# x's rows for the last sums: sixteen indexed transfers issued by GpSimd in place of four direct loads issued by SyncE

## The chip, the cores and the metric

One core of one Trainium2 chip runs the whole program. The metric is the device time of one execution in microseconds (us). A core has TensorE (PE, matmuls; PEld is its weight loads), VectorE (DVE), ScalarE (ACT), GpSimd (POOL) and SyncE (SP). SP here only issues transfers, and POOL issues some beside its arithmetic. All transfers run on 16 DMA engines that the core's queues share.

## The reference

A layer of graph attention over 2048 nodes of width 256, with 8 heads of width 32, in float32:

```
h   = relu(layernorm(x))                                   # source rows
hs, ht = masked layernorms of h and of h_target, with scale and bias
q, k, v = ht @ Wq + bq (divided by sqrt 32), hs @ Wk + bk, hs @ Wv + bv
p   = softmax over the sources of q.k where adj != 0
ht  = layernorm(ht + (p @ v) @ Wo + bo), masked
out = x + ht + gelu(ht @ W1) @ W2
```

What the change is about is the first term of the last line: the raw rows of x are wanted a second time, at the very end.

## The kernel before, in words

The 2048 targets are cut into 4 chunks of 512 columns (4 tiles of 128 rows, `TILES`). There are three stages.

**Projections.** x and h_target come in, are normalised and turned, and give keys, queries and values. The buffer of x is given to other tensors afterwards. The keys are split into a high and a low part for the matmuls, and copies of keys, values and queries are saved to memory for a rare general path that a flag chooses (the flag is 0 here).

**Attention.** For every chunk, group of 4 heads and tile of sources, PE makes scores, DVE masks them into a ring `probs` of 12 buffers, ACT takes the exponential, and PE multiplies by the values. POOL adds some of the exponentials up (`add_up`) and loads the mask's rows (`load_adj`). The sums of a chunk go to memory, come back packed, are inverted by DVE (`invert`), are stored again, and are then broadcast by SP over the partitions into `inverse` (`spread_inverse`, L394 to L403: 2 transfers of 256 KB, one per group of heads, in which each of 4 source rows is repeated for 32 partitions). For the last chunk DVE multiplies the context by it (`divide_last`, L1153), and PE's `attend(LAST)` (L1465) waits for that product.

**The last stage.** For each chunk c in turn PE runs `widen` (8 steps of 6 matmuls, W1), `turn_y` (transposes for the next chunk), `narrow` (8 steps of 6 matmuls, W2), and within `widen(c)`, at its third step, `turn_out(c - 1)` (L1577: 8 transposes of the finished chunk before). `attend(LAST)` stands between `narrow(0)` and `widen(1)`. ACT takes the two gelus of each step; DVE makes the low part of each (`split_gelu`, L1099), and between them the normalisation of later chunks (`y_stats`, `y_root`, `y_apply`), `join(c)` (L1104) for which `turn_out(c)` waits, and `finish(c)` (L1112), which adds x's rows from the buffer `xr` and writes `result`. Every engine runs its list in the order in which it is written, and the waits are on counted semaphores. `finish(0)` stands in DVE's list behind the second `split_gelu` of chunk 1. `narrow(1)` waits for `finish(0)`, as both use the accumulator `acc`.

`xr` holds one chunk's rows: 128 partitions by 4 tiles by 256 values, over the space of the keys, and so SP loads it first when the copies of the keys are saved (L467 to L469), then again behind the stores of each chunk (L480). At the end of POOL's list, behind the attention, stand two multiplications and additions over the last chunk of the residual (`make_residual(LAST, ...)`, L564), which wait for the low half of chunk 0's activations (`y_lo_out`), and then only the reading of the flag.

Of the kernel before, what the change touches and what calls it, by code (L numbers as in the profile page):

```python
# [5 lines left out]
F32 = mybir.dt.float32  # L6
F32R = mybir.dt.float32r
BF16 = mybir.dt.bfloat16
I32 = mybir.dt.int32
U16 = mybir.dt.uint16  # L10
ACT = mybir.ActivationFunctionType
ALU = mybir.AluOpType
AX_X = mybir.AxisListType.X

P = 128
# [8 lines left out]
TILES = CHUNK // P  # L24
# [8 lines left out]
def graph_attention(nc, x, adj, nodemask, h_target, ln1_scale, ln1_bias, Wq, bq, Wk, bk, Wv, bv, Wo, bo,  # L33
                    ln2_scale, ln2_bias, W1, W2, out):
    S, D = x.shape
    FF = W1.shape[1]
    NCH = S // CHUNK
    ST = S // P
# [6 lines left out]
    NT = NCH * GT  # L45
# [16 lines left out]
    x_rows = x.rearrange("(n p) d -> p n d", p=P)  # L62
# [13 lines left out]
    with ExitStack() as ctx:  # L76
        def sb(name, shape, dt, scope=ctx):
            return scope.enter_context(nc.sbuf_tensor(name, shape, dt))

        def sem(name):  # L80
            return ctx.enter_context(nc.semaphore(name))
# [30 lines left out]
        largest_all = sb("largest_all", [P, 1], F32)  # L112
        largest_one = sb("largest_one", [1, 1], F32)
        flag = sb("flag", [1, 1], I32)
        sums = sb("sums", [P, NCH, PACK], F32)
        inverses = sb("inverses", [P, NCH, PACK], F32)
        wo = sb("wo", [P, DC, D], F32)
# [11 lines left out]
        with ExitStack() as late:  # L129
            g_hi = sb("g_hi", [P, FC, CHUNK], F32R, late)  # L130
            g_lo = sb("g_lo", [P, FC, CHUNK], F32R, late)
            xr = sb("xr", [P, TILES, D], F32, late)
            out_T = sb("out_T", [P, DC, CHUNK], F32, late)
            g_full = sb("g_full", [P, 2, CHUNK], F32, late)
            result = sb("result", [P, TILES, D], F32, late)
# [43 lines left out]
        with ExitStack() as late:  # L179
            yT_hi = sb("yT_hi", [P, DC, CHUNK], F32R, late)  # L180
            yT_lo = sb("yT_lo", [P, DC, CHUNK], F32R, late)
            yT = [sb(f"yT{i}", [P, DC, CHUNK], F32, late) for i in range(2)]
        probs = sb("probs", [P, RING, 2, CHUNK], F32, att)
        added_up = sb("added_up", [P, PAIRS, 2, CHUNK], F32, att)
        sums_wide = sb("sums_wide", [P, CHUNK], F32, att)
# [19 lines left out]
        columns_made = sem("columns_made")  # L205
        node_row_in = sem("node_row_in")
        made = sem("made")
        beta_masked = sem("beta_masked")
        nodes_made = sem("nodes_made")
        row_tested = sem("row_tested")  # L210
# [25 lines left out]
        kept = sem("kept")  # L236
# [13 lines left out]
        used = sem("used")  # L250
# [32 lines left out]
        x_again = sem("x_again")  # L283
# [3 lines left out]
        summed = sem("summed")  # L287
# [31 lines left out]
        def rows_of(c):  # L319
            return slice(c * TILES, (c + 1) * TILES)  # L320
# [50 lines left out]
        def _(sp):  # L371
# [92 lines left out]
                    sp.dma_start(v_saved, V[:]).then_inc(kept, 16)  # L464
            store_sums(LAST, 1)
            pack_sums(LAST)
            sp.wait_ge(used, NT)  # L467
            sp.wait_ge(kept, 16 * 3)
            sp.dma_start(xr[:], x_rows[:, rows_of(0), :]).then_inc(x_again, 16)  # L469
            spread_inverse(LAST)  # L470
            def store_last(ts, ds, results):
                sp.wait_ge(summed, TILES * LAST + results)
# [2 lines left out]
            for c in range(LAST):  # L475
                for half in range(2):
                    ts = slice(half * TILES // 2, (half + 1) * TILES // 2)
                    sp.wait_ge(summed, TILES * c + (half + 1) * TILES // 2)
                    sp.dma_start(out_rows[:, rows_of(c), :][:, ts, :], result[:, ts, :]).then_inc(stored, 16)
                sp.dma_start(xr[:], x_rows[:, rows_of(c + 1), :]).then_inc(x_again, 16)  # L480
                if c == LAST - 1:
                    sp.wait_ge(ht_kept, 16)
                    sp.wait_ge(q_kept, 32 * NCH)
                    general = load_flag(sp, "sp")
# [33 lines left out]
        def _(pool):  # L518
            def load_adj(c, t):
                n = c * TILES + t  # L520
                if n >= 2:
# [8 lines left out]
            pool.dma_start(vec_rows[NV - ST:NV, :], nodemask.rearrange("(n p) -> n p", p=P)).then_inc(nodes_in, 16)  # L530
            pool.dma_start(node_row[:], nodemask.rearrange("(o s) -> o s", o=1).to_broadcast([P, S])
                           ).then_inc(node_row_in, 16)
            pool.wait_ge(x_in[2], 16)
            load_adj(0, 0)
            pool.wait_ge(x_in[3], 16)
# [28 lines left out]
            def make_residual(c, step):  # L564
                h = htn[:, rows_of(c), :]
                if step == 0:
                    if c == 0:
                        pool.wait_ge(rest_made, 2)
                        pool.wait_ge(ht_kept, 16)
                    nc.gpsimd.tensor_tensor(h, h, gamma1_row[:, None, :].to_broadcast(wide), ALU.mult  # L570
                                            ).then_inc(residual, 1)
                else:
                    pool.wait_ge(residual, 2 * c + 1)
                    nc.gpsimd.tensor_tensor(h, h, rest_row[:, None, :].to_broadcast(wide), ALU.add
                                            ).then_inc(residual, 1)
# [23 lines left out]
            pool.wait_ge(y_lo_out, DC)  # L599
            make_residual(LAST, 0)  # L600
            make_residual(LAST, 1)

            general = load_flag(pool, "pool")
            with pool.If(general):
# [257 lines left out]
        def _(dve):  # L862
# [247 lines left out]
                                            ).then_inc(joined, 1)  # L1110

            def finish(c):  # L1112
                dve.wait_ge(x_again, 16 * (c + 1))
                if c:
                    dve.wait_ge(stored, 32 * c)
                for t in range(TILES):
                    n = c * TILES + t
                    dve.wait_ge(out_turned, 2 * c + t // 2 + 1)
                    nc.vector.scalar_tensor_tensor(out=result[:, t, :], in0=acc4[:, t, :], scalar=nodes[:, n:n + 1],
                                                   in1=xr[:, t, :], op0=ALU.mult, op1=ALU.add).then_inc(summed, 1)  # L1120

            def finish_last():
                def join_part(d, at, width):
                    ts = slice(at, at + width)
                    nc.vector.tensor_tensor(out_T[:, d, ts], acc[:, d, ts], yT[LAST % 2][:, d, ts], ALU.add
                                            ).then_inc(joined, 1)

                def result_part(t, d):
                    n, ds = LAST * TILES + t, slice(d * P, (d + 1) * P)
                    nc.vector.scalar_tensor_tensor(out=result[:, t, ds], in0=slot4[0][:, t, ds], scalar=nodes[:, n:n + 1],  # L1130
                                                   in1=xr[:, t, ds], op0=ALU.mult, op1=ALU.add).then_inc(summed, 1)

                dve.wait_ge(out_turned, 2 * LAST)
                dve.wait_ge(narrowed, DC * LAST + 1)
                join_part(0, 0, CHUNK)
                dve.wait_ge(x_again, 16 * NCH)
                dve.wait_ge(stored, 32 * LAST)
                dve.wait_ge(out_turned, 2 * LAST + 1)
                for t in range(TILES):
                    result_part(t, 0)  # L1140
                dve.wait_ge(narrowed, DC * NCH)
                for half in range(2):
                    join_part(1, half * CHUNK // 2, CHUNK // 2)
                for half in range(2):
                    dve.wait_ge(out_turned, 2 * LAST + 2 + half)
                    for t in range(half * TILES // 2, (half + 1) * TILES // 2):
                        result_part(t, 1)
# [530 lines left out]
```

## Time and profile before

| | us |
|---|---|
| median of 3 runs | 491.21 (490.66 to 491.3) |
| span of the profiled execution | 488.1 |
| PE busy in the span | 472.1 (97%) |
| DVE busy | 418.4 (86%) |
| ACT busy | 376.5 (77%) |
| POOL busy | 305.6 (63%) |

The profile shows one execution, from its first to its last instruction: the span. What lies around it (start and end of the program) is in the median and not in the span, and no time of its own is given for the profiled execution beside its span, so the median less the span, 3.1 us, stands for that part. PE is busy nearly throughout; its granted clock is 0.998 over the span. A busy figure is an average over all stages. The change is in the last stage, which begins at about 376 us.

### The profile page before, as it was taken

The numbers are of one execution on the slowest core, as the hardware profiler recorded it, in microseconds if no ns is written. First come the engines' busy times: TensorE is split into PE (matmuls) and PEld (weight loads), VectorE is DVE, ScalarE is ACT, GpSimd is POOL, SyncE is SP. The second block draws the span as 40 slices with busy tenths as digits, with TensorE's granted clock in tenths as the row PEclk, the third lists the DMA queues.
The fourth block names the chain that finished last, engine by engine and source line by source line (L and its number), as shares of the span: only waits on it lengthen the run. The fifth ranks groups of instructions, "written<-read, shape, count | busy, mean of one in ns | idle before, by whom it ended". The sixth has DMA issues, their size and how long they took to land.

```text
span 488.1 us, 10628 instructions
## 1 busy us (share of the span) xinstructions
PE 472.1 (97%) x4366; PEld 243.2 (50%) x4366; DVE 418.4 (86%) x631; ACT 376.5 (77%) x462; POOL 305.6 (63%) x152
## 2 busy tenths in 40 slices
PE   3999989999999999999999999999999999999995
PEld 1557533343333333343333333343435888888884
DVE  6889499999999999999999999999997977566243
ACT  4887979998998998998998998999995571727150
POOL 1000019977998999999999998999998300000000
PEclk9999999999999999999999999999999999999999
DMA  8997879925432673232763400500000100202021
GB/s 231 243 217 133 157 216 385 346 47 109 172 69 47 76 173 58 44 52 50 77 177 57 77 2 3 186 35 1 2 2 1 46 33 13 87 1 86 1 87 45
DMA packets 53775, 46.93 MB, mean 96 GB/s; under 512 B 35486, under 2 KB 46652, under 8 KB 53212
## 3 DMA queue, kind: packets, MB, share of 16 engines
q1 hardware_dynamic: 51216, 37.30, 28.7%
q0 software_dynamic: 2480, 8.92, 10.4%
q8 instruction: 35, 0.57, 0.5%
q14 instruction: 16, 0.13, 0.1%
q10 hardware_dynamic: 28, 0.01, 0.0%
HBM read 31.93 MB, written 14.81 MB: 96 GB/s over the span
## 4 chain that ended last, share of the span: by engine, by line
PE 72%; DVE 11%; issue 9%; ACT 4%; POOL 3%; DMA 1%; DVEq 0%; POOLq 0%
PE acc L1434 18%; PE slot L1419 16%; PE acc L1452 8%; DVE probs L1044 8%; PE slot L1536 3%; PE slot L1534 3%; PE slot L1535 3%; PE slot L1322 3%; PE acc L1571 2%; PE acc L1573 2%; PE acc L1572 2%; PE slot L1485 2%; POOL added_up L554 2%; DVE stats L865 1%; PE slot L1342 1%
## 5 line engine op out<-in xcount | busy, mean ns | idle before, releaser
L1044 DVE SCALAR_TENSOR_TENSOR probs<-maskT,slot 128x1024 f32<-128x1024 uint16 x256 | 298.0, 1217 | 6.1 <-PE slot L1419 5.7
L759 ACT ACTIVATE probs<-probs 128x1024 f32<-128x1024 f32 x256 | 266.8, 1057 | 22.3 <-DVE probs L1044 4.8
L554 POOL TENSOR_TENSOR added_up<-added_up,probs 128x1024 f32<-128x1024 f32 x96 | 226.8, 2411 | 0.2
L1434 PE MATMUL acc<-probs,V 128*32 128x512 f32 x1024 | 136.3, 604 | 1.8 <-DVE q_lo_staged L970 1.8
L1452 PE MATMUL acc<-probs,ones 128*32 128x256 f32 x1024 | 77.0, 379 | 0.0
L1452 PEld LDWEIGHTS acc<-probs,ones 128*32 128x32 f32 x1024 | 33.3, 110 | 72.8 <-issue 71.2
L1419 PE MATMUL slot<-q_hi,k_hi 32*128 32x512 f32 x512 | 64.4, 493 | 0.9 <-DVE probs L1044 0.3
L823 ACT ACTIVATE g_full<-slot 128x512 f32<-128x512 f32 x32 | 19.3, 602 | 45.2 <-issue 30.0
L1419 PEld LDWEIGHTS slot<-q_hi,k_hi 32*128 32x128 f32 x512 | 24.5, 181 | 59.1 <-DVE probs L1044 54.4
L551 POOL TENSOR_TENSOR added_up<-probs 128x1024 f32<-128x1024 f32 x16 | 38.1, 2406 | 24.9 <-ACT probs L759 15.0
L1419 PE MATMUL slot<-q_lo,k_hi 32*128 32x512 f32 x512 | 51.8, 391 | 0.0
L1419 PE MATMUL slot<-q_hi,k_lo 32*128 32x512 f32 x512 | 51.3, 389 | 0.0
L1434 PEld LDWEIGHTS acc<-probs,V 128*32 128x32 f32 x1024 | 20.3, 108 | 48.7 <-issue 46.0
L523 POOL DMA_DIRECT2D adj_raw<-in_adj x16 | 8.9, 559 | 49.5 <-DMA maskT<-adj_raw 38.0
L1101 DVE TENSOR_TENSOR g_lo<-g_full,g_hi 128x512 fp32r<-128x512 f32 x32 | 23.0, 718 | 17.4 <-ACT g_hi L824 17.3
L1419 PEld LDWEIGHTS slot<-q_lo,k_hi 32*128 32x128 f32 x512 | 24.7, 183 | 4.7
L1534 PE MATMUL slot<-yT_hi,w_hi 128*128 128x512 f32 x64 | 25.6, 399 | 0.0
L1536 PE MATMUL slot<-yT_hi,w_lo 128*128 128x512 f32 x64 | 25.0, 390 | 0.0
L1535 PE MATMUL slot<-yT_lo,w_hi 128*128 128x512 f32 x64 | 24.9, 389 | 0.0
L1419 PEld LDWEIGHTS slot<-q_hi,k_lo 32*128 32x128 f32 x512 | 24.9, 184 | 0.0
L824 ACT ACTIVATE g_hi<-slot 128x512 fp32r<-128x512 f32 x32 | 19.1, 597 | 0.0
L1571 PE MATMUL acc<-g_hi,w_hi 128*128 128x512 f32 x48 | 18.9, 394 | 0.0
(144 smaller groups left out, 496.6 us busy)
## 6 DMA issues: line engine op xcount, KB each, us to landing
adj_raw<-in_adj POOLq DMA_DIRECT2D x16, 512.0 KB, 5.5
htn<-in_L_gnn_h_target SPq DMA_DIRECT2D x4, 512.0 KB, 7.4
ht_saved<-htn SPq DMA_DIRECT2D x1, 2048.0 KB, 8.1
k_hi_saved<-k_hi SPq DMA_DIRECT2D x1, 2048.0 KB, 10.2
k_lo_saved<-k_lo SPq DMA_DIRECT2D x1, 2048.0 KB, 14.5
v_saved<-V SPq DMA_DIRECT2D x1, 2048.0 KB, 8.9
inverse<-inverse_saved SPq DMA_DIRECT2D x8, 256.0 KB
maskT<-in_L_gnn_W SPq DMA_DIRECT2D x2, 1024.0 KB, 6.4
```

What stands on the lines that cost most here:

```text
L551: nc.gpsimd.tensor_tensor(added_up[:, pair], at(ADDED[0]), at(i), ALU.add).then_inc(added, 1)
L554: nc.gpsimd.tensor_tensor(added_up[:, pair], added_up[:, pair], at(i), ALU.add).then_inc(added, 1)
L759: nc.scalar.activation(p, p, ACT.Exp).then_inc(exped, 1)
L1044: nc.vector.scalar_tensor_tensor(out=probs[:, u % RING], in0=m, scalar=-HALF_EDGE, in1=slot[u % SLOTS][:], op0=ALU.add, op1=ALU.min).then_ ...
L1101: nc.vector.tensor_tensor(g_lo[:, f, :], g_full[:, f % 2, :], g_hi[:, f, :].bitcast(F32), ALU.subtract).then_inc(gelu_lo, 1)
L1419: mm = pe.matmul(slot[(PAIRS * k + j // 2) % SLOTS][:, j % 2, :], keys_part[head, g, i * P:(i + 1) * P], queries_part[head, g, :], start=( ...
L1434: mm = pe.matmul(acc[HD * j:HD * j + HD, 0, :], V[:, i, h * HD:(h + 1) * HD], probs[:, (PAIRS * k + j // 2) % RING, j % 2, :], start=(i == 0),
L1452: mm = pe.matmul(acc[HD * j:HD * j + HD, 1, ts], ones[:], probs[:, (PAIRS * k + j // 2) % RING, j % 2, ts], start=first and not half, stop ...
L1534: pe.matmul(dst, w1_hi[:, d, fs], yT_hi[:, d, :], start=(d == 0), stop=False)
L1535: pe.matmul(dst, w1_hi[:, d, fs], yT_lo[:, d, :], start=False, stop=False)
L1536: mm = pe.matmul(dst, w1_lo[:, d, fs], yT_hi[:, d, :], start=False, stop=(d == DC - 1))
L1571: pe.matmul(dst, w2_hi[:, f, ds], g_hi[:, f, :], start=(f == 0), stop=False)
```

## The change

`xr` becomes four times as large and holds all 16 tiles of x. It leaves the space of the keys for that of the `probs` ring. POOL makes a table of row numbers at the start (`iota`), and behind its two residual steps issues one indexed transfer for each tile of 128 rows, each with one row number per partition. SP's first load and its two waits, and its three loads behind the stores, are gone. `finish(0)` waits for all sixteen transfers; the later chunks and `finish_last` wait for no load.

```diff
+        row_index = sb("row_index", [P, ST], U32)
...
-            xr = sb("xr", [P, TILES, D], F32, late)
...
             yT = [sb(f"yT{i}", [P, DC, CHUNK], F32, late) for i in range(2)]
+            xr = sb("xr", [P, ST, D], F32, late)
...
             pack_sums(LAST)
-            sp.wait_ge(used, NT)
-            sp.wait_ge(kept, 16 * 3)
-            sp.dma_start(xr[:], x_rows[:, rows_of(0), :]).then_inc(x_again, 16)
             spread_inverse(LAST)
...
-                sp.dma_start(xr[:], x_rows[:, rows_of(c + 1), :]).then_inc(x_again, 16)
...
+            nc.gpsimd.iota(row_index[:], pattern=[[P, ST]], base=0, channel_multiplier=1).then_inc(index_made, 1)
             pool.wait_ge(x_in[2], 16)
             load_adj(0, 0)
...
             make_residual(LAST, 0)
             make_residual(LAST, 1)
+
+            pool.wait_ge(index_made, 1)
+            pool.wait_ge(used, NT)
+            pool.wait_ge(kept, 16 * 3)
+            for n in range(ST):
+                pool.indirect_dma_start(
+                    out=xr[:, n, :], out_offset=None, in_=x,
+                    in_offset=bass.IndirectOffsetOnAxis(ap=row_index[:, n:n + 1], axis=0)).then_inc(x_again, 16)
...
             def finish(c):
-                dve.wait_ge(x_again, 16 * (c + 1))
+                if c == 0:
+                    dve.wait_ge(x_again, 16 * ST)
...
-                                                   in1=xr[:, t, :], op0=ALU.mult, op1=ALU.add).then_inc(summed, 1)
+                                                   in1=xr[:, n, :], op0=ALU.mult, op1=ALU.add).then_inc(summed, 1)
...
             def finish_last():
...
-                                                   in1=xr[:, t, ds], op0=ALU.mult, op1=ALU.add).then_inc(summed, 1)
+                                                   in1=xr[:, n, ds], op0=ALU.mult, op1=ALU.add).then_inc(summed, 1)
...
-                dve.wait_ge(x_again, 16 * NCH)
```

## Rows read from the trace of the kernel before

**Rows 1.** The profile's first page, busy time of each engine
```profile
PE 472.1 (97%) x4366; PEld 243.2 (50%) x4366; DVE 418.4 (86%) x631; ACT 376.5 (77%) x462; POOL 305.6 (63%) x152
```
**Rows 2.** Busy time by stretch: PE, PEld, DVE, ACT, POOL, PE's clock, DMA share, GB/s
```profile
410.00:430.00 20.00, 20.00 (x99) 16.80 (x98) 14.18 (x31) 11.38 (x20) 0.00 (x0) 1.00 0.17 54
382.00:384.00 2.00, 2.00 (x11) 1.74 (x11) 2.00 (x3) 2.00 (x4) 0.00 (x0) 1.00 0.75 233
398.65:404.10 5.45, 5.45 (x26) 4.52 (x25) 2.55 (x4) 3.39 (x6) 0.00 (x0) 1.00 0.25 96
316.00:320.00 4.00, 4.00 (x52) 1.57 (x52) 4.00 (x5) 3.82 (x6) 4.00 (x2) 1.00 0.28 102
```
**Rows 3.** Waits from 395 to 488 us: engine, line <- releaser: total, times, longest
```profile
DVE g_lo L1101 <- ACT g_hi L824: 17.3, 25, 1.8
DVE context L1158 <- DMA inverse<-inverse_saved: 2.0, 1, 2.0
```
**Rows 4.** What touches the tile xr: durations in ns min/median/max, first and last start
```profile
L480 SPq DMA_DIRECT2D xr<-in_x x3: 500/503/505, 418.4 to 465.5; - x3
L469 SPq DMA_DIRECT2D xr<-in_x x1: 401/401/401, 380.8 to 380.8; - x1
...
DMA to landing us min/median/max: 3.9/3.9/4.2
```
**Rows 5.** POOL's instructions in order: start, duration, line, operation
```profile
2.58 0.56 POOL L531 DMA_DIRECT2D node_row<-in_nodemask  x1
12.90 0.53 POOL L523 DMA_DIRECT2D adj_raw<-in_adj  x1 [9.76 <-DMA xs<-in_x]
...
26.87 0.53 POOL L523 DMA_DIRECT2D adj_raw<-in_adj  x1 [11.18 <-DMA maskT<-adj_raw]
...
387.43 2.40 POOL L574 TENSOR_TENSOR htn<-htn,rest_row 128x1024 f32<-128x1024 f32 x1
```
**Rows 6.** The line of POOL's direct loads, durations in ns
```profile
L523 POOL DMA_DIRECT2D adj_raw<-in_adj x16: 530/570/593, 12.9 to 256.0; - x16
```
**Rows 7.** SP's queue in order of time
```profile
395.55 0.61 SPq L396 DMA_DIRECT2D inverse_saved<-inverses  x1
397.44 1.14 SPq L402 DMA_DIRECT2D inverse<-inverse_saved  x2
```
**Rows 8.** The page's list of transfers: size, median us to landing
```profile
out<-result SPq DMA_DIRECT2D x7, 256.0 KB, 2.2
```
**Rows 9.** DVE in order of time, 388 to 418 us
```profile
388.80 1.57 DVE L1101 TENSOR_TENSOR g_lo<-g_full,g_hi 128x512 fp32r<-128x512 f32 x1
...
392.66 0.69 DVE L1101 TENSOR_TENSOR g_lo<-g_full,g_hi 128x512 fp32r<-128x512 f32 x1
...
404.78 1.29 DVE L1158 TENSOR_TENSOR context<-context,inverse 128x512 f32<-128x512 f32 x2 [2.02 <-DMA inverse<-inverse_saved]
...
411.52 1.28 DVE L1109 TENSOR_TENSOR out_T<-acc,yT 128x512 f32<-128x512 f32 x2
...
416.28 1.65 DVE L1119 SCALAR_TENSOR_TENSOR result<-acc,nodes,xr 128x256 f32<-128x256 f32 x4
```
**Rows 10.** PE and ACT in order of time
```profile
393.94 0.59 ACT L824 ACTIVATE g_hi<-slot 128x512 fp32r<-128x512 f32 x1
...
395.03 0.39 PE L1534 MATMUL slot<-yT_hi,w_hi 128*128 128x512 f32 x1
...
408.16 3.61 PE L1485 MATMUL slot<-wo,context 128*128 128x256 f32 x16
...
414.36 1.04 PE L1581 MATMUL acc<-ident,out_T 128*128 128x128 f32 x8
...
424.21 0.48 PE L1571 MATMUL acc<-g_hi,w_hi 128*128 128x512 f32 x1
```
**Rows 11.** DVE beside POOL's load of 26.87 us
```profile
26.85 0.16 DVE L876 TENSOR_TENSOR newton<-rstd 128x4 f32<-128x4 f32 x1
27.05 0.16 DVE L878 SCALAR_TENSOR_TENSOR newton<-spread,newton 128x4 f32<-128x4 f32 x1
```

More of the change, by code:

```diff
@@ L9 @@
 I32 = mybir.dt.int32
+U32 = mybir.dt.uint32
 U16 = mybir.dt.uint16
@@ L207, in graph_attention @@
         made = sem("made")
+        index_made = sem("index_made")
         beta_masked = sem("beta_masked")
```

## The prediction, made before the changed kernel was run

> **What bounds the kernel now.** I looked first at the busy shares: PE is busy 472.1 of 488.1 us and no other engine comes near [rows 1]. Then at the stage that the change touches, by stretches: from 410 to 430 us PE is busy all 20.00 us at full clock, DVE 14.18, ACT 11.38, POOL 0.00, and the DMA engines 0.17 of the time [rows 2]. So PE sets the pace there, each instruction behind the last, and a change counts only if it makes PE wait or takes a wait from it. Then the waits of that stage: DVE waits for ACT in small pieces, 25 times, 17.3 us in all, and once 2.0 us for the broadcast of the inverse sums; nobody waits for `xr` [rows 3, 4]. What I need beyond that is how far each thing that PE waits for is ahead of PE, and for that I read single instructions in order of time.
>
> **What the change removes.** SP's four issues cost it 0.40 us once and 0.50 us three times, their data lands 3.9 us after the issue, and nothing waits for it [rows 4]. The first stands at 380.8, and SP's next work begins at 395.55, when the sums are inverted [rows 4, 7]; the three others stand behind stores and in front of an idle queue. The two waits taken from SP and the two kinds of wait taken from DVE were satisfied long before. So the removal gives 0.0 us on PE's path. What hides it is SP's idle time, and if that were gone it would be 0.5 us for each load at the most.
>
> **What it adds early.** One table-making instruction on POOL behind the issue of 2.58 us. POOL then idles 9.76 us before its load of 12.90 [rows 5]. The trace has no such instruction; it makes 16 values per partition, and the bounds are 0 and the 2.40 us of a POOL instruction over 1024 values [rows 5]. Either way it is hidden: 0.0 us. The new place of `xr` costs nothing that I can find, as the `probs` ring is dead when POOL reaches the transfers, and their waits (`used`, `kept`, the table) are met by then.
>
> **What it adds late.** POOL ends its residual step at 387.43 + 2.40 = 389.83 and now issues 16 transfers of 128 rows of 1 KB, 128 KB each. Only the reading of the flag is queued behind them, at the end of the program. The trace has no indexed transfer. Its nearest rows are POOL's direct loads over 128 partitions, 0.57 us each, one right behind the other where two are issued [rows 5, 6]; this is the lower end. The upper end is 2.40 us, POOL's instruction over a whole tile [rows 5]. An indexed transfer must fetch a number per row and make an address of it, which the direct one doesn't, and so I take twice the direct one, 1.1 us: nearer the row of its own kind. Then the last is issued at 389.83 + 16 x 1.1 = 407.4, and with some 2.5 us to land (2.2 for a store of 256 KB [rows 8]) all of x is there at 409.9. `finish(0)` starts at 416.28 [rows 9], so this adds no wait. It could even start later: PE needs its 1.65 us done only at 424.21, when `narrow(1)` starts [rows 9, 10], that is a start at 422.6. The wait begins to cost when POOL's pitch exceeds (422.6 - 2.5 - 389.83) / 16 = 1.89 us.
>
> **What these transfers collide with.** At 397.44 SP issues the broadcast of the inverse sums, 2 x 256 KB, and the wait for it ends at 404.78 [rows 7, 9]. Its data moves from about 398.65 to 404.1 at 96 GB/s with a DMA share of 0.25; the same broadcast one chunk earlier shows 102 GB/s and 0.28 over 4 us, while x's direct load of the same size shows 233 GB/s and 0.75 [rows 2]. A share that stays at a quarter, at a steady rate, in a transfer that nothing else disturbs, reads as 4 of 16 engines that are full, rather than 16 that idle three quarters of the time. The Trainium skill says how this comes: on the page "DMA: Bandwidth & Descriptors", section "Rules for kernel authors", a transfer whose outermost dimension has fewer than 16 entries is confined to at most that many engines, and here the outermost has 4 heads. The share of 0.25 agrees. If the rule did not hold here, x would run in the idle three quarters and the collision would cost nothing, which is the rival "hidden" below.
>
> With full engines x's packets delay it. Per busy engine the broadcast moves 96 / (16 x 0.25) = 24 KB per us, x's load 233 / (16 x 0.75) = 19.4. An indexed transfer puts 128 / 16 = 8 KB on each engine: 0.33 us at the first rate, 0.41 at the second. At one per 1.1 us this is 0.30 to 0.38 of each engine's time, all through the broadcast. Its 5.45 us become 5.45 / 0.70 = 7.8 to 5.45 / 0.62 = 8.8, which is 2.35 to 3.35 us more. Those four engines run at the higher rate, so I take 2.4, and 0.2 for the small store of 395.55 ahead of it, which now stands among x's packets (bounds 0 and 0.4, one transfer's share): the broadcast lands D = 2.6 us later.
>
> Who waits? DVE, which waits already, is late by all of D. Its list from 404.78 to 412.80 (`divide_last`, statistics, the root, `join(0)`) has no gap, so `join(0)` ends at 412.80 + D, and `turn_out(0)` on PE, at 414.36 now, has 1.56 us to spare [rows 9, 10]. `attend(LAST)`, at 408.16, with the product ready at 406.07, has 2.09 to spare: the earlier stall is 2.6 - 2.09 = 0.5 and is part of the later one. PE loses D - 1.56 = 1.0 us, and as PE runs without a gap from there to the end, the end moves by it. DVE's own lateness is then made good in its gaps [rows 3].
>
> **The sum.** 488.1 + 0.0 (removed) + 0.0 (table) + 0.0 (wait of `finish(0)`) + 1.0 (collision) = 489.1 of span, and with the 3.1 us around it 492.2; from the median, 491.21 + 1.0 = 492.2. For the collision's bounds: at the lower end of 0.57 us per transfer POOL is done at 399.0 and x is through at about 401, so the broadcast shares its engines for only 2.3 us at a share of 0.7: D = 1.7, cost 0.1. At 1.5 us the share is 0.22 to 0.27, D is 1.5 to 2.0, cost 0 to 0.5. At 1.1 us and the slower packets D is 3.4 to 3.8, cost 1.8 to 2.2. Less than nothing is not to be had, as nothing on PE's path goes.
>
> **The rivals.**
>
> Hidden: the collision costs less than the 1.56 us that PE has in hand, because a DMA engine fills the gaps of one queue with packets of the other, or because the pitch is near the direct one or near 1.5 us. For it: even the direct load of x shows engines busy only 0.75. Against it: the four engines of the broadcast show no gap. Time 491.2, not slower than before; it decides for D under 1.56 us. Chance 0.22.
>
> Late x: POOL needs more than 1.89 us for each transfer, and then `finish(0)` holds `narrow(1)`. At 2.1 us: 389.83 + 33.6 + 2.5 = 425.9, 3.3 us after 422.6, time 494.5. At the upper end of 2.40: 430.7, 8.1 us late, 499.3. For it: software makes these transfers and it must read an index for each row. Against: it would be over three times the direct load. The Trainium skill speaks for this rival too: "DMA: Bandwidth & Descriptors", "Anatomy of one DMA", gives a transfer from GpSimd a fixed 2.0 us beside its bytes; if the fixed part were paid one after the other, the sixteen would be an estimated 32 us by that page and land late. The direct issues here are over after 0.57 us each [rows 6], which speaks against its being paid so on POOL. Chance 0.12.
>
> Port: POOL and DVE keep each other from memory. The low part of a gelu takes 1.57 us at 388.80 beside POOL's residual step, against 0.69 at 392.66 [rows 9]. If sixteen indexed transfers do the same, DVE's chain from 390.37 to the split at 392.66 and the gelu that ends at 394.53 has only 0.5 us in hand before the matmul of 395.03 [rows 10]. One split that is 0.88 late costs 0.4 us, and if each of DVE's eight two-input instructions there is held so, 8 x 0.88 - 0.5 = 6.5 us. Against it: tiny instructions of DVE keep their 0.16 us and their pitch of 0.20 beside POOL's direct load at 26.87 [rows 5, 11]. Time 491.6 to 497.7. The Trainium skill has the rule on the page "SBUF — State Buffer", section "Who interferes with whom": a VectorE instruction with two inputs in SBUF contends with a GpSimd instruction that reads it. An indexed transfer reads its row numbers there, the direct one reads nothing. Chance 0.06.
>
> Gain: the freed queue and the loads that don't stand beside the last chunks' stores bring 0.6 us or more. I find no instruction that waits for either. Time 490.6. Chance 0.05.
>
> **How the numbers follow.** The forecast (a broadcast late, PE held at `turn_out(0)` for 1.0 us) has 0.55, with its own range of 491.4 to 493.4. Its time is 492.2. About 0.2%, 1.0 us, is what a measurement of this kernel can tell from no change, and the forecast lies on that line: I give 0.33 of its 0.55 to slower and 0.22 to the same. Hidden adds 0.21 to the same and 0.01 to faster, late x 0.11 to slower and 0.01 to the same, port 0.05 and 0.01, gain 0.05 to faster. Together: faster 0.06, same 0.45, slower 0.49. The range is 490.8 to 495.3: it holds the forecast, hidden, and the mild half of late x and port.
>
> **What would show it.** The wait of DVE's `divide_last` for the broadcast grows from 2.0 to some 4.6 us, and the DMA share between 398.6 and 406 rises from 0.25 to about 0.6. POOL shows 16 instructions of about 1.1 us from 389.8 to 407. PE shows a first gap of about 0.5 us before `attend(LAST)` and another before `turn_out(0)`, 1.0 us together, and none before `narrow(1)`. A pitch above 1.9 us and a gap in front of `narrow(1)` would prove late x; splits of more than 0.7 us between 390 and 407, port; a broadcast that lands at 404.8 to 406.3, hidden. I'm wrong outright if PE stalls in front of anything else, or the time falls below 490.8.

## The result, and the profile after

The changed kernel takes 492.68 us (median; 491.84 to 495.31), the kernel before in the same session 490.66 (490.11 to 493.08). The ratio is 1.0039, 95% interval [1.0022, 1.0056]: slower by 1.9 us. The forecast was 492.2 and 1.0 us, so the cost is 0.9 us above it.

The profile shows where it goes, if one thing is taken off first. In this execution everything was already 0.29 us late before POOL's first indexed transfer: the low part of a gelu that began at 388.80 [rows 9] begins at 389.09. That belongs to the attention, which the change doesn't touch, and is called the offset below. Every "later" is after it is taken off.

POOL in order of time, changed kernel (start, duration, instruction, idle time before it):
```profile
387.72 2.41 POOL L574 TENSOR_TENSOR htn<-htn,rest_row 128x1024 f32<-128x1024 f32 x1
390.28 1.29 POOL L607 DMA_INDIRECT xr<-in_x,row_index  x1 [0.16 <-issue]
...
394.79 1.59 POOL L607 DMA_INDIRECT xr<-in_x,row_index  x1 [0.30 <-issue]
...
400.83 0.95 POOL L607 DMA_INDIRECT xr<-in_x,row_index  x1 [0.30 <-issue]
402.08 0.96 POOL L607 DMA_INDIRECT xr<-in_x,row_index  x1 [0.30 <-issue]
...
411.14 0.95 POOL L607 DMA_INDIRECT xr<-in_x,row_index  x1 [0.30 <-issue]
```
Sixteen transfers in 20.86 us from the first start to the last, 1.39 from one to the next on the mean and 1.26 during the broadcast; a good fifth of it is a gap of 0.30 us behind each.

SP's queue, then two stretches: 410 to 430 as in [rows 2], and the eight microseconds of the broadcast:
```profile
395.85 0.61 SPq L399 DMA_DIRECT2D inverse_saved<-inverses  x1
398.35 1.14 SPq L405 DMA_DIRECT2D inverse<-inverse_saved  x2
```
```profile
410.00:430.00 20.00, 19.68 (x96) 16.35 (x95) 14.92 (x41) 11.37 (x20) 1.78 (x2) 1.00 0.15 48
399.30:407.30 8.00, 8.00 (x37) 6.63 (x36) 2.20 (x4) 3.03 (x5) 5.90 (x7) 1.00 0.48 157
```
The broadcast is issued 398.35 - 397.44 - 0.29 = 0.62 us later [rows 7], since it waits for the small store to land. From its issue to the start of `divide_last` it then takes 9.71 us where it took 7.34, 2.37 more, so its 5.45 us of data have become some 7.8, in a stretch whose DMA share is 0.48 and not 0.25 [rows 2].

DVE, then PE, in order of time:
```profile
389.09 1.58 DVE L1109 TENSOR_TENSOR g_lo<-g_full,g_hi 128x512 fp32r<-128x512 f32 x1
...
398.73 0.69 DVE L1109 TENSOR_TENSOR g_lo<-g_full,g_hi 128x512 fp32r<-128x512 f32 x1 [0.29 <-issue]
...
408.06 1.29 DVE L1166 TENSOR_TENSOR context<-context,inverse 128x512 f32<-128x512 f32 x2 [5.00 <-issue]
...
414.92 1.28 DVE L1117 TENSOR_TENSOR out_T<-acc,yT 128x512 f32<-128x512 f32 x2
...
418.45 1.65 DVE L1128 SCALAR_TENSOR_TENSOR result<-acc,nodes,xr 128x256 f32<-128x256 f32 x4
```
```profile
409.50 3.69 PE L1493 MATMUL slot<-wo,context 128*128 128x256 f32 x16 [0.83 <-DVE context L1166]
...
416.26 1.09 PE L1589 MATMUL acc<-ident,out_T 128*128 128x128 f32 x8 [0.33 <-DVE out_T L1117]
...
426.17 0.48 PE L1579 MATMUL acc<-g_hi,w_hi 128*128 128x512 f32 x1
```
`divide_last` begins D = 408.06 - 404.78 - 0.29 = 2.99 us later. PE gets two gaps, 0.83 before `attend(LAST)` and 0.33 before `turn_out(0)`. (They make up less than PE's lateness, because a matmul otherwise begins before the modelled end of the one before it: `attend(LAST)` begins 409.50 - 408.16 - 0.29 = 1.05 us later and `turn_out(0)` 1.61.) It reaches `narrow(1)` 426.17 - 424.21 - 0.29 = 1.67 us later, which is inside the interval of the ratio (1.1 to 2.7 us). `finish(0)` waits for nothing, and no gap stands in front of `narrow(1)`.

### The profile page after: what moved, and what is told of

It reads as the page before. It is cut to its first block, busy times and chain, and to the rows that moved or that the text cites. A ratio compares the mean times of both kernels' runs of the same rounds, so it can differ in the third digit from the quotient of the medians.

```text
span 490.3 us, 10641 instructions
## 1 busy us (share of the span) xinstructions
PE 473.4 (97%) x4366; PEld 243.4 (50%) x4366; DVE 418.5 (85%) x631; ACT 376.5 (77%) x462; POOL 323.1 (66%) x169
## 4 chain that ended last, share of the span: by engine, by line
PE 66%; DVE 15%; issue 10%; ACT 4%; POOL 3%; DMA 2%; DVEq 0%; SPq 0%; POOLq 0%
PE acc L1442 18%; PE slot L1427 16%; PE acc L1460 8%; DVE probs L1052 8%; PE slot L1330 3%; POOL added_up L554 2%; PE slot L1544 2%; PE slot L1542 2%; PE slot L1543 2%; DVE stats L873 2%; PE slot L1493 1%; PE acc L1580 1%; PE acc L1581 1%; PE acc L1579 1%; PE slot L1350 1%
## 5 line engine op out<-in xcount | busy, mean ns | idle before, releaser
L607 POOL DMA_INDIRECT xr<-in_x,row_index x16 | 17.2, 1077 | 4.7 <-issue 4.7
```

## The experiments

All ran timed against the kernel before. D is the lateness of `divide_last` and "PE's loss" that of `narrow(1)`, both with that run's own offset taken off (read at the gelu of 388.80 [rows 9], in experiment 2 at that of 392.66; at that of 388.80 both of its figures would be 0.07 us more). In the texts on record, where letters stand, A is the collision of x's packets with the broadcast, and C a second mechanism that the traces brought up: late updates of TensorE's counters.

**1. The changed kernel again.** No edit.

> The changed kernel again, as the measure for its neighbours. Theory A (the indexed transfers share the four engines of the inverse broadcast; DVE's divide_last, join(0) and then PE are late): ratio to before 1.004 (1.003 to 1.005), divide_last starts about 408.0 against 404.8, x lands before finish(0) wants it. Rival B (POOL's sixteen instructions themselves disturb DVE or the program as a whole, wherever they stand): the same time, so it isn't told apart here.

Measured: 492.51 against 491.16, ratio 1.0037 [1.0020, 1.0053]. D is 3.23, PE's loss 1.87. The effect repeats.

**2. Direct transfers in the place of the indexed ones.**
```diff
-                pool.indirect_dma_start(out=xr[:, n, :], ..., in_offset=...)
+                pool.dma_start(xr[:, n, :], x_rows[:, n, :]).then_inc(x_again, 16)
```


> In place of the sixteen indexed transfers POOL issues sixteen direct ones of the same rows, at the same place. Theory A: only the traffic matters. POOL is done in 16 x 0.57 = 9.1 us, at 399.5, and 2 MB are through by about 401, so the broadcast (data from about 399) shares its engines for 2 us at a share near 0.7: it lands 1.4 us later for that and the small store 0.6 us later, D = 2.0, PE loses 0.4: ratio 1.001 (1.000 to 1.002). Theory that it is the indexing that costs (reading row numbers, POOL's long instructions): ratio 1.000, nothing late. Theory that all GpSimd transfers cost alike, whatever their pitch: 1.004.

Measured: ratio 1.0002 [0.9992, 1.0012]. POOL, then three stretches, then DVE, of this kernel:
```profile
390.99 8.77 POOL L607 DMA_DIRECT2D xr<-in_x  x16
```
```profile
398.00:400.00 2.00, 2.00 (x14) 1.75 (x12) 1.43 (x3) 2.00 (x5) 1.76 (x4) 1.00 0.87 244
400.00:402.00 2.00, 2.00 (x11) 1.63 (x10) 1.10 (x2) 2.00 (x5) 0.00 (x0) 1.00 0.54 153
402.00:404.00 2.00, 2.00 (x11) 1.65 (x10) 1.34 (x2) 1.32 (x2) 0.00 (x0) 1.00 0.25 92
```
```profile
407.98 1.29 DVE L1164 TENSOR_TENSOR context<-context,inverse 128x512 f32<-128x512 f32 x2 [3.93 <-DMA inverse<-inverse_saved]
```
The same bytes, issued by 399.8: the DMA share falls from 0.87 to the broadcast's own 0.25 while the broadcast is still on its way. D = 407.98 - 404.78 - 1.29 = 1.91 (this run's offset is 1.29), PE's loss 0.49. SP issues the broadcast at 399.80, so 399.80 - 397.44 - 1.29 = 1.07 of D is the small store's and only 0.84 the broadcast's own. This is the lower end of the prediction's bounds (D 1.7, cost 0.1), a little above it. So the place alone isn't the cost: it is how long x's packets stand beside the broadcast.

**3. The indexed transfers behind the broadcast.** One wait more on POOL, and a counter for each chunk of x, so that `finish(c)` waits for four transfers only.
```diff
+            pool.wait_ge(inverses_in, 16 * GROUPS * NCH)
             for n in range(ST):
...
-                dve.wait_ge(x_again, 16 * ST)
+                dve.wait_ge(x_again[c], 16 * TILES)
```


> POOL waits until the broadcast has landed and only then issues the sixteen indexed transfers; each chunk of x has a counter of its own, so that finish(0) waits for the first four only. Theory A: the broadcast lands at 405.0 as in the kernel before, the first four are issued by 405 + 4 x 1.35 = 410.4 and land by 413, ahead of finish(0) at 416.3; the others land by 430, ahead of finish(1) at 439.8. Ratio 1.000 (0.999 to 1.001). Rival B: POOL is as busy as in the changed kernel, only later, beside DVE's root and join: ratio 1.003 to 1.005.

Measured: 499.97 us, ratio 1.0170 [1.0153, 1.0188]. A clear miss. The collision is gone as expected, yet the kernel is 8.3 us slower. Its rows, DVE and ACT and PE in order of time, then three stretches:
```profile
406.21 1.29 DVE L1167 TENSOR_TENSOR context<-context,inverse 128x512 f32<-128x512 f32 x2 [1.94 <-DMA inverse<-inverse_saved]
...
418.78 1.66 DVE L1128 SCALAR_TENSOR_TENSOR result<-acc,nodes,xr 128x256 f32<-128x256 f32 x4 [0.90 <-remote]
...
425.53 0.69 DVE L1110 TENSOR_TENSOR g_lo<-g_full,g_hi 128x512 fp32r<-128x512 f32 x1 [5.09 <-issue]
```
```profile
424.42 0.60 ACT L832 ACTIVATE g_full<-slot 128x512 f32<-128x512 f32 x1 [7.26 <-remote]
...
430.07 0.60 ACT L832 ACTIVATE g_full<-slot 128x512 f32<-128x512 f32 x1 [4.57 <-remote]
```
```profile
425.55 0.50 PE L1543 MATMUL slot<-yT_hi,w_hi 128*128 128x512 f32 x1 [3.19 <-issue]
...
431.20 0.80 PE L1543 MATMUL slot<-yT_hi,w_hi 128*128 128x512 f32 x1 [3.56 <-ACT g_hi L833]
```
```profile
424.00:426.00 2.00, 0.45 (x2) 0.41 (x3) 0.47 (x1) 1.08 (x2) 1.66 (x2) 1.00 0.53 160
426.00:428.00 2.00, 1.64 (x6) 0.78 (x4) 0.23 (x1) 0.00 (x0) 1.20 (x2) 0.64 0.31 90
428.00:430.00 2.00, 0.00 (x0) 0.00 (x0) 0.00 (x0) 0.00 (x0) 0.00 (x0) 0.50 0.26 66
```
ACT waits 7.26 us for a step of matmuls that has long ended. "Remote" says that no instruction near it explains the wait. The trace also records each step of each counter, and there the reason stands. PE's own steps, usually 0.01 to 0.02 us behind the end of the matmul, arrive late:

| kernel | matmul ends | its counter steps |
|---|---|---|
| before, `narrow(0)` | 407.64, 408.32 | 407.66, 408.34 |
| changed, `narrow(0)` | 407.99, 408.67 | 413.43, 414.18 |
| changed, `attend(LAST)` | 413.19 | 414.35 |
| experiment 3, `turn_out(0)` | 416.47, 416.91 | 418.68, 419.42 |
| experiment 3, `widen(1)` | 418.29, 419.64, 421.00 | 424.39, 430.04, 430.12 |

So there is a second mechanism (C): in a long row of indexed transfers, PE's counter steps get stuck, up to 10 us here (steps and ends are matched in their order). The waits are real ones: ACT begins 0.03 us after the steps of 424.39 and 430.04. PE goes on until it must wait for a slot, and stops for 3.19 and for 3.56 us. Between the two stops its granted clock falls from 1.00 to 0.50, the lower of its two levels, 1.2 of 2.4 GHz, and stays there in every stretch up to 436. `narrow(1)` comes 9.8 us late in this execution: the two stops make 6.75 us of it, and most of the rest is matmuls that take 0.63 us where they took 0.39.

**4. The broadcast as eight transfers of one head.** The indexed ones stay where the change put them, and `divide_last` counts the eight.
```diff
+                if c == LAST:
+                    for h in range(HEADS):
+                        g, j = h // PER, h % PER
+                        head = inverse_saved[h:h + 1, cols_of(c)]
+                        sp.dma_start(inverse[HD * j:HD * j + HD, g, :], head.to_broadcast([HD, CHUNK])
+                                     ).then_inc(inverses_in, 16)
+                    return
```


> The changed kernel, but the last broadcast is made of eight transfers of one head each (1 row repeated for 32 partitions, 64 KB) in place of two of four heads. Theory A in the form that the broadcast of four heads is held by four engines: the eight use all sixteen, and the DMA share of that stretch is no longer capped; their issue takes 8 x 0.57 = 4.6 us from 398.3, the last is issued at 402.9 and lands by 405.5: D = 0.4 us, PE loses nothing: ratio 1.000 (0.999 to 1.001). If the number of engines doesn't matter (all packets queue alike): D stays near 3 us or grows by the issue time, ratio 1.004 or more.

Measured: ratio 1.0018 [1.0006, 1.0030]: half of the cost is left. Two stretches, then DVE, then PE:
```profile
400.00:402.00 2.00, 2.00 (x11) 1.65 (x10) 1.12 (x2) 2.00 (x4) 1.51 (x2) 1.00 0.66 194
402.00:404.00 2.00, 2.00 (x11) 1.65 (x10) 0.69 (x1) 0.37 (x1) 1.57 (x2) 1.00 0.74 232
```
```profile
404.83 1.29 DVE L1173 TENSOR_TENSOR context<-context,inverse 128x512 f32<-128x512 f32 x2 [1.73 <-DMA inverse<-inverse_saved]
414.25 1.29 DVE L1124 TENSOR_TENSOR out_T<-acc,yT 128x512 f32<-128x512 f32 x2 [2.44 <-remote]
```
```profile
414.18 0.48 PE L1551 MATMUL slot<-yT_hi,w_lo 128*128 128x512 f32 x1 [0.25 <-issue]
415.59 1.09 PE L1596 MATMUL acc<-ident,out_T 128*128 128x128 f32 x8 [0.23 <-DVE out_T L1124]
```
Over all engines the same bytes find room: D is 404.83 - 404.78 - 0.32 = -0.27, although x's transfers run at the same pitch. That shows the collision and its remedy. What is left is C: `join(0)` could start at about 411.8 and waits 2.44 us for the steps of `narrow(0)`, which arrive at 414.23 and 414.27 for ends at 407.98 and 408.66. PE's loss is 0.99. In the changed kernel the same steps arrive at 414.18, and `join(0)` starts at 414.92: there the broadcast is the later one by 0.7, and C stands hidden just behind it.

**5. The indexed transfers ahead of the residual steps.** The loop is moved above `pool.wait_ge(y_lo_out, DC)`.

> POOL issues the sixteen indexed transfers ahead of its two residual steps, as soon as the attention is through (about 377 us), and so is done by 377 + 21 = 398, before the inverse broadcast (398 to 404) has begun. Theory A (the collision with the broadcast is all there is): D under 1 us, no PE stall, ratio 1.000 (0.999 to 1.001). Theory C (from the run that waited for the broadcast: some 9 us into a row of indexed transfers, TensorE's counter updates begin to arrive up to 6 us late, until the transfers' traffic ends): the updates that tell ACT that a step of widen(0) is ready, 387 to 396.5 us, come late, ACT and then PE starve as in that run: ratio 1.010 to 1.020.

Measured: ratio 1.0007 [0.9997, 1.0018]. POOL issues from 377.86 to 401.3; the steps of matmuls that ended at 395.33, 396.69 and 397.56 arrive at 397.41, 401.22 and 402.70. DVE in order of time:
```profile
402.37 1.95 DVE L1110 TENSOR_TENSOR g_lo<-g_full,g_hi 128x512 fp32r<-128x512 f32 x1 [3.12 <-issue]
404.24 3.48 DVE L1105 TENSOR_TENSOR yT_lo<-yT,yT_hi 128x512 fp32r<-128x512 f32 x2
407.64 1.28 DVE L1167 TENSOR_TENSOR context<-context,inverse 128x512 f32<-128x512 f32 x2
```
C also strikes elsewhere in the stage. The first late step is that of 395.33, 17 us after the first transfer; in experiment 3 it is that of 416.47, 9 us after it. Neither theory's forecast holds. The median loses 0.3 us (-0.1 to 0.9) and not the 1.010 to 1.020 of C. But the trace isn't free of loss either, as A had it: D is 407.64 - 404.78 - 0.15 = 2.71 and PE's loss 1.28, more than the median shows, and why this execution lost more than the median stays open. `divide_last` waits for no broadcast here. It stands behind DVE's own work, which the late steps held up, and whose two-input instructions then took 1.95 us, and 3.48 for two, beside POOL's residual steps (now at 401.36 to 406.57), where each took 0.69 before.

**6. Behind the broadcast, and a wait after every four until they have landed.** As 3, with
```diff
+                if n and n % TILES == 0:
+                    pool.wait_ge(x_again[n // TILES - 1], 16 * TILES)
```


> As the run in which POOL waits for the broadcast (1.017), but after every four indexed transfers POOL also waits until they have landed. So never more than four are under way. Theory C1 (the late TensorE updates come of many indexed transfers in a row or under way at once): no update is late, finish(0) starts at 416 to 418, ratio 1.000 (0.999 to 1.002). Theory C2 (any indexed transfer beside PE's updates makes them late, however few): late updates again, ratio 1.008 to 1.02.

Measured: ratio 1.0001 [0.9988, 1.0014]. Every step on record of PE's counters is on time (that for the end at 418.56 is missing, but ACT begins at 418.60), PE's loss is 0.0.

**7. Rows of 512 bytes.** The same loop fetches half rows, and both halves of the sums add the same one.
```diff
-                    out=xr[:, n, :], out_offset=None, in_=x,
+                    out=xr[:, n, 0:P], out_offset=None, in_=x.rearrange("s (t d) -> (s t) d", t=2),
```


> The changed kernel, but each indexed transfer brings rows of 512 bytes instead of 1024 (half of x's values; other rows than the right ones, and both halves of the result add the same half). Theory A by bytes: a transfer takes 0.17 to 0.21 us of each engine, a share of 0.13 to 0.16 at a pitch of 1.3 us, so D = 0.8 to 1.0 plus at most 0.6 for the small store: D = 1.5 at most, PE loses nothing, ratio 1.000 to 1.001. If the number of packets or the issue itself counts, not the bytes: D stays at 3.0, ratio 1.004. Theory C adds: if the late TensorE updates come of the number of indexed transfers and not of their bytes, those of narrow(0) (408 us) are still late by 5 us and join(0) waits for them, until about 414: ratio 1.002.

Measured: ratio 1.0015 [1.0005, 1.0024]. DVE in order of time:
```profile
406.33 1.29 DVE L1167 TENSOR_TENSOR context<-context,inverse 128x512 f32<-128x512 f32 x2 [3.11 <-DMA inverse<-inverse_saved]
414.10 1.29 DVE L1117 TENSOR_TENSOR out_T<-acc,yT 128x512 f32<-128x512 f32 x2 [0.80 <-remote]
```
Half the bytes at the same pitch (POOL's durations are those of the whole rows): D falls from 2.99 to 406.33 - 404.78 - 0.45 = 1.10. The steps are as late as before (408.10 ends, 414.08 arrives), so C hangs on the number of indexed transfers or on their time, not on the bytes, and it is what `join(0)` waits for now. PE's loss is 0.73, although D is below PE's slack: here that loss is C's.

**8. All of x in one direct load by SP, at the old place.** POOL issues nothing.
```diff
+            sp.dma_start(xr[:], x_rows).then_inc(x_again, 16)
```


> The large buffer and the single wait stay, but SP brings all of x in one direct transfer of 2 MB at the place of its first load (380.8 us); POOL issues nothing. It lands after some 9 us, by 391, before the small store of 395.6. Theory A: nothing collides, ratio 1.000 (0.999 to 1.001), divide_last at 404.8. If the large buffer's place or the loads taken from behind the stores mattered: a ratio that differs from 1.000 by more than 0.001 either way.

Measured: ratio 0.9997 [0.9984, 1.0010]. The freed slots of SP's queue and the missing waits bring nothing in the trace: `narrow(1)` starts at 424.51, which is 424.51 - 424.21 - 0.29 = 0.01 us later than before. The ratio's interval alone would still hold the 0.6 us of the rival "gain".

**9. As 6, but a wait only after eight.** `n % TILES` becomes `n % 8`.

> As the paced run that was as fast as the kernel before (POOL starts after the broadcast), but POOL waits for the landing only once, after eight transfers. Sixteen in a row gave 1.017, four in a row 1.000. If it takes eight or more in a row before TensorE's updates come late (they were late from the eighth on in the run of sixteen): the first eight, 406 to 416, do no harm or little, and the second eight, from about 418.5 to 429, little: ratio 1.000 to 1.003. If the delay needs only more than four: late updates in 411 to 417 or 424 to 430, ratio 1.005 to 1.012.

Measured: ratio 1.0007 [0.9993, 1.0021]. POOL in order of time:
```profile
416.07 1.13 POOL L610 DMA_INDIRECT xr<-in_x,row_index  x1 [0.30 <-issue]
419.23 0.95 POOL L610 DMA_INDIRECT xr<-in_x,row_index  x1 [2.03 <-DMA xr<-in_x,row_index]
```
This pause of 2.03 us is nearly all that sets it apart from experiment 3, and the time is 8 us shorter. The steps are on time (ends at 408.97 and 416.28, steps at 408.98 and 416.29).

**10. 32 direct transfers of half rows behind the broadcast, in a row.**
```diff
+                for half in range(2):
+                    ds = slice(half * P, (half + 1) * P)
+                    pool.dma_start(xr[:, n, ds], x_rows[:, n, ds]).then_inc(x_again[n // TILES], 16)
```


> POOL starts after the broadcast and issues 32 direct transfers of half rows (64 KB each) in a row, with no pacing: 32 x 0.57 = 18 us, about as long as the sixteen indexed ones took (20.4 us, ratio 1.017), and twice as many. If any long row of GpSimd transfers makes TensorE's updates late: ratio over 1.005, updates of widen(1), 415 to 424, late by microseconds. If it belongs to the indexed kind: all updates within 0.1 us of their matmuls, ratio 1.000 (0.999 to 1.001).

Measured: ratio 1.0001 [0.9988, 1.0014]. POOL is busy 17.05 us on end, about as long as with the sixteen indexed ones, and PE's steps are on time (ends at 409.24 and 416.55, steps at 409.26 and 416.56). A long row of transfers doesn't do it; a long row of indexed ones does.

**11. Both remedies at the change's own place:** the broadcast of 4, and the wait of 6 after every four.

> The changed kernel's place (POOL starts at 390.3), with both cures: the last broadcast as eight transfers of one head (sixteen engines), and POOL waiting after every four indexed transfers for their landing. If the broadcast's four engines and the late TensorE updates are the whole of the loss: divide_last at 404.0 to 405.5, the updates of narrow(0) at 408.7 on time, no PE stall, ratio 1.000 (0.999 to 1.001). If a third cost exists: 1.001 or more.

Measured: ratio 1.0012 [1.0002, 1.0023], a slight miss. DVE in order of time:
```profile
405.15 1.29 DVE L1175 TENSOR_TENSOR context<-context,inverse 128x512 f32<-128x512 f32 x2 [1.91 <-DMA inverse<-inverse_saved]
```
D is 405.15 - 404.78 - 0.47 = -0.10, the steps are on time and PE's loss is 0.0. The trace thus shows nothing of the 0.6 us in the ratio; the profiled execution took 490.83, 0.2 over the median of before. What the rest is stays open.

**12. The pacing alone, with the old broadcast.** The fourth corner of that square.

> The sixteen indexed transfers stand where the change put them, the last broadcast is the old one, and POOL waits after each four until they have landed. This is the fourth corner of a square: broadcast old or spread, transfers in a row or by fours. Both theories expect TensorE's counter updates on time, as in the other kernels that pace by four. Collision: the second four, from about 398.7 to 403.4, meet the broadcast; four times 0.33 to 0.41 us and some 0.6 for the small store make D 1.9 to 2.2 us, against 2.98 in a row, so that PE loses about 0.6 to 0.9 us, and the ratio is 1.0018 to 1.003. Late updates: if they and not the broadcast had set the changed kernel's end, the ratio would be that of the spread and paced kernel, 1.0012, although D is still near 2 us.

Measured: ratio 1.0032 [1.0016, 1.0049]. DVE, then PE, in order of time:
```profile
407.73 1.29 DVE L1168 TENSOR_TENSOR context<-context,inverse 128x512 f32<-128x512 f32 x2 [4.53 <-DMA inverse<-inverse_saved]
```
```profile
409.17 3.69 PE L1495 MATMUL slot<-wo,context 128*128 128x256 f32 x16 [0.40 <-DVE context L1168]
...
415.93 1.09 PE L1591 MATMUL acc<-ident,out_T 128*128 128x128 f32 x8 [0.31 <-DVE out_T L1119]
...
425.86 0.48 PE L1581 MATMUL acc<-g_hi,w_hi 128*128 128x512 f32 x1
```
The steps are on time (an end at 408.09, its step at 408.10). D is 407.73 - 404.78 - 0.43 = 2.52, more than the 1.9 to 2.2 expected (0.58 of it is the small store's, and four transfers cost the broadcast 1.94 and not 1.5), and PE's loss 425.86 - 424.21 - 0.43 = 1.22. The ratio is slightly above the range too. It decides between the theories all the same:

| kernel | PE's steps | D | PE's loss | D less loss |
|---|---|---|---|---|
| 2, direct | on time | 1.91 | 0.49 | 1.42 |
| 12, paced | on time | 2.52 | 1.22 | 1.30 |
| changed | late | 2.99 | 1.67 | 1.32 |
| 1, changed again | late | 3.23 | 1.87 | 1.36 |

PE's loss is D less 1.3 to 1.4 whether the steps are late or not. In the changed kernel the whole cost comes through the broadcast; the late steps add nothing there and would keep about 1.0 us of it (experiment 4) if the broadcast alone were mended. No kernel tried beats the kernel before; 2, 5, 6, 8, 9 and 10 can't be told from it.

## Why the prediction was right, point by point

**What is removed: 0.0.** Right. Experiment 8 leaves out the three later loads and their waits and PE is where it was; it keeps a load at the place of the first one.

**The table: 0.0.** Right: POOL makes it in 0.17 us at 3.22, in its early idle time.

**POOL's pitch: 1.1 us.** Mis-sized. One transfer takes 0.95 to 1.59 us, and I had not thought of a gap between two: 0.30 us each time, so 1.26 in the steady part and 1.39 on the mean. The last is through at 412.1 and not at 407.4. The limit of 1.89 us was not reached, x had landed by 413.9, and `finish(0)` at 418.45 had time: "late x" is refuted. The Trainium skill, "DMA: Bandwidth & Descriptors", section "Anatomy of one DMA", has the fixed 2.0 us of a GpSimd transfer; one every 1.26 us shows that it isn't paid one after the other.

**The collision: four engines, shared.** Right in mechanism, place and nearly in size. The broadcast's own delay is 2.99 less the 0.62 of its later issue, 2.37, where I took 2.4. By the formula of the prediction 5.45 / (5.45 + 2.37) = 0.70, so x takes 0.30 of each of the four engines. At a pitch of 1.26 that is 0.38 us for each transfer, inside my 0.33 to 0.41. Two of my errors nearly cancel here: the packets were heavier than the value taken and came less often. That 2.37 came so near to 2.4 is in part luck. The sign "DMA share about 0.6" was worked out wrongly: it adds x's share to all sixteen engines, also to the four that are full. With x on the other twelve alone it is 0.25 + 0.75 x 0.30 = 0.475, and 0.48 was measured. The prediction's D of 1.5 to 2.0 at a pitch of 1.5 us leaves out the small store, too; with it, it is 1.5 to 2.4. Half the bytes (7) and a broadcast over all engines (4) take most or all of it away, so "hidden" is refuted, in the form that engines fill their gaps with another queue's packets. Where the broadcast isn't confined, the DMA share rises to 0.66 and 0.74 in experiment 4; by the Trainium skill's rule on the outermost dimension ("DMA: Bandwidth & Descriptors", "Rules for kernel authors") that is so because each transfer now has 32 entries outermost where it had 4, and the trace agrees.

**The small store: 0.2, bounds 0 and 0.4.** Wrong, and the largest part of the miss: it lands 0.62 us later, beyond my upper bound. I had charged it one transfer's share of an engine. In experiment 12, where POOL stood still between 396.5 and 398.6, it was 398.45 - 397.44 - 0.43 = 0.58 late as well, so four transfers issued before suffice, and with the denser direct ones (2) it was 1.07. Where it waits I did not separate.

**DVE and PE: D less 1.56.** The slack was measured rightly, but the chain behind `divide_last` grew: `join(0)` starts 3.11 us later where `divide_last` starts 2.99 later, and PE takes up work 0.12 us later than the difference. The effective slack is 1.3. The gaps stand where I put them, 0.83 and 0.33 us for "0.5 and another", and none before `narrow(1)`.

**The sum.** Predicted 2.4 + 0.2 - 1.56 = 1.0. Measured 2.37 + 0.62 + 0.12 + 0.12 - 1.56 = 1.67 in the profile and 1.9 in the ratio. The 3.1 us that the prediction puts around the span are not all start and end: in every execution timed since, the time is 1.6 to 1.8 us above the span. The rest is that the profiled execution of the kernel before was a fast one. It cancels in the difference of the two kernels.

**Port.** Refuted for the indexed transfers: the gelus' low parts keep their 0.69 us beside indexed transfers (398.73), and the one of 1.58 us stands beside POOL's residual step as it did before. What slows such an instruction is the residual step, as experiment 5 shows where it stands elsewhere. The Trainium skill's rule in "SBUF — State Buffer", "Who interferes with whom", doesn't show in an indexed transfer, though this one reads its row numbers there.

**What I didn't see.** Mechanism C. "Wrong outright if PE stalls in front of anything else" did not happen in the changed kernel, but by 0.7 us only, and in a kernel that looks like the obvious cure (3) C costs 8.3 us.

## What to carry to other kernels

A transfer that fills only some of the DMA engines is exposed to what the other queues bring: before moving traffic beside it, read its DMA share, and either spread it over all engines or see how much slack its reader has, counted to the engine that sets the pace. When one limit is removed, look at what was second: here curing the broadcast alone gave back only half, as TensorE's late counter steps stood 0.7 us behind. A wait that is put down to "remote" or "issue" on an instruction whose producer has long ended deserves a look at the time at which the counter itself stepped.

## What the runs showed of the hardware

Indexed transfers on GpSimd in long rows delay the counter steps of TensorE's matmuls. Sixteen in a row did it in all six traces that had them (the changed kernel's, and experiments 1, 3, 4, 5 and 7), by up to 10 us and until 2 to 4 us after the last indexed transfer was issued; four or eight and then a wait for their landing did it in none (6, 9, 11, 12), nor did 16 or 32 direct ones (2, 10). Bytes don't matter (7). What path the two share, and why it begins 9 us after the first transfer in one kernel and 17 in another, stays open; so does whether it goes by the number of indexed transfers outstanding or by their time on end. The slower time is not that of the traced execution alone: all five of experiment 3 took 498.4 to 501.9 us. Yet a part of the recording itself isn't ruled out. In these six traces and in that of experiment 6, 18 to 29 ends of instructions, nearly all of ACT and DVE and all after the first indexed transfer, have no counter step on record; in those of the kernel before and of experiments 2 and 8 to 12 every end of ACT, DVE and PE in the last stage has its own. A missing step need not be a late one: in experiment 6 ACT begins 0.04 us after the end of 418.56, whose step is missing.

An indexed transfer of 128 rows costs GpSimd 0.95 to 1.59 us (once 2.83, in experiment 5) and a gap of 0.30, whether its rows have 1024 or 512 bytes; the direct one costs 0.55 (8.77 / 16) without a gap.

In experiment 3 TensorE stood still for 3.2 us up to 425.55. Its granted clock was 1.00 up to 426, 0.64 from 426 to 428 and 0.50 from 428 to 436; the second stop, of 3.6 us, began when it had already fallen. In the kernels without such a stop (9, 11) it was 1.00 throughout these stretches.
